# Stores of three phases of a graph network kernel moved from SyncE's queue to ScalarE's

## The chip, the cores and the metric

The kernel runs on one core of one Trainium2 chip. The metric is the device time of one execution in microseconds (us), the median of several runs. The core's engines are TensorE (PE, with its weight loads as PEld), VectorE (DVE), ScalarE (ACT), GpSimd (POOL) and SyncE (SP), each with an instruction stream of its own. They wait for each other by semaphores. Transfers run on 16 DMA engines that the whole core shares.

## The reference, cut to what matters

There are 50,000 nodes with 128 features and 12,500 edges `src -> dst`, sorted by `dst`. Four graph layers follow each other, each as `x = layernorm(x + layer(x))`:

```python
x = _layernorm(x + _L0_gnn_ref(x, edge_index, edge_attr_8, ...))       # attention over the edges
x = _layernorm(x + _L1_gnn_ref(x, edge_index, edge_type_16, ...))      # messages, mean, own layernorm
x = _layernorm(x + _L2_gnn_ref(x, node_vec1, src, dst, edge_attr_4, edge_attr_8, ...))  # equivariant
x = _layernorm(x + _L3_gnn_ref(x, edge_index, ...))                    # hypergraph convolution, batch norm
```

The first layer computes a softmax over the edges of each target and a weighted sum of values; the second a relu of a linear map of source features and edge type, averaged per target; the third gated products of source features and edge attributes, summed per target; the fourth two hypergraph convolutions with a batch norm between.

## The kernel before, in words

Nodes that no edge touches follow a formula of their own (class `Dense`), whose work is sprinkled over the phases. What this case is about are the states of the edges' endpoints. Each phase reads a table in memory with one row of 128 floats for each edge's target (rows 0 to 12,499) and one for its source (the next 12,500), and writes the next table: the attention phase reads `x` and writes T1, the message phase reads T1 and writes T2, the equivariant phase reads T2 and writes T3, and the tail phase reads T3. Between two phases stands a barrier of all engines, and SP does not reach it before all stores of its phase have landed (`sp.wait_ge(s_st[i], ...)`).

Each of the three phases handles the edges in 25 chunks (`NC`) of 500 (`CE`), four tiles (`CT`) of 125 (`TP`). For every chunk POOL gathers source rows (helper `gathers`, line 438), PE turns them and multiplies, ACT copies PSUM and applies functions, DVE does the running sums along the sorted edges, adds the residual, and takes statistics of both rows' norms. Then ACT's `root` takes the square root, DVE's `scale` the reciprocal, and ACT's `norm` (`norm2` in the message phase) writes the normalized rows: eight ACTIVATEs into `y[c % 2]`, four for the targets, four for the sources. `y` has two buffers, so the norm of chunk c waits until the stores of chunk c-2 have landed: `need(act, s_st[c % 2], 32 * (c // 2))`. A store of a chunk, `store(c)`, is two DMAs of 250 KB, 500 rows of 512 bytes each.

The order is written out by hand. Every engine has a loop over steps `s`, and in a step it works on several chunks: what stands as `live(s - 3): norm(s - 3)` is done in step s for chunk s-3. A step of one engine may run at another time than the same step of another engine.

- Attention: ACT (loop at L706) does `outF(s-1)`, `targets`, `query`, `sources` of s+2, `norm(s-2)`, `exps(s+1)`, `root(s-1)`. SP (L542) loads bias and penalties of chunk s+2 and a piece of `xT` for the dense part, then `store(s-2)`.
- Message: ACT (L1437) does `outF(s-1)`, `source(s+2)`, a root, `norm1(s-2)`, `message(s+1)`, `dn.squares` (L1022), a root, `norm2(s-3)`. SP (L1303) loads types, masks and target rows, then `store(s-3)`, and behind it `dn.load_turned` (L1012), the `xT` that `dn.squares` reads.
- Equivariant: ACT (L1737) does `source(s+1)` (L1714, `eq_xs`), `features(s+1)` (L1720 and L1721), `norm(s-3)` (L1734), `gate(s+2)` (L1709, `eq_sg`) and `root(s-2)` (L1726, `eq_sd`). SP (L1613) does `load_scalars(s+3)`, `load_attr(s+1)`, `load_mask(s+1)` (`eq_same`, one row spread over 128 partitions), `load_targets(s)` (`eq_z`) and `store(s-4)` (L1610, L1611).

The waits that bind these loops in the equivariant phase: DVE's `hidden(c)` waits for `gate(c)`; PE's `net(c+1)` waits for `hidden(c)`; PE's `turn` stands behind `net`; ACT's `source` waits for `turn`.

Of the kernel before, what the change touches and what calls it, by code (L numbers as in the profile page):

```python
# [27 lines left out]
N, D, E = 50000, 128, 12500  # L28
# [3 lines left out]
CT = 4  # L32
CE = CT * TP
# [437 lines left out]
def live(c):  # L471
    return 0 <= c < NC


def attention_phase(nc, g, K, T, dn):

    with ExitStack() as ctx:
# [40 lines left out]
        @block.sync  # L518
        def _(sp):
            for n in W:  # L520
                sp.dma_start(W[n][:], g[n]).then_inc(s_w, 16)
            sp.dma_start(bo[:], g["rowv"][0:1, :].broadcast_to([TP, D])).then_inc(s_w, 16)
            sp.dma_start(sel[:], g["sel"]).then_inc(s_w, 16)
            sp.dma_start(spread[:], g["spread"]).then_inc(s_w, 16)
            sp.wait_ge(s_init, 2)
            sp.dma_start(srcI[:], g["src_col"]).then_inc(s_w, 16)
            sp.dma_start(dstI[:], g["dst_col"]).then_inc(s_w, 16)

            def load_pen(c):
                need(sp, s_args, c - 1)  # L530
                sp.dma_start(pen[c % 2][:], T["dpen"][:, CE * c:CE * c + CE].broadcast_to([D, CE])).then_inc(s_pen[c % 2], 16)

            def load_bias(c):
                need(sp, s_att, c - 1)
                sp.dma_start(eb[c % 2][0:8, :], g["ea8T"][:, CE * c:CE * c + CE]).then_inc(s_eb[c % 2], 16)

            def store(c):
                sp.wait_ge(s_y, c + 1)
                sp.dma_start(rows_of(T["T1"], CE * c, CT), y[c % 2][:, 0:CT, :]).then_inc(s_st[c % 2], 16)
                sp.dma_start(rows_of(T["T1"], CE * c + E, CT), y[c % 2][:, CT:2 * CT, :]).then_inc(s_st[c % 2], 16)  # L540

            for s in range(-2, NC + 2):  # L542
                if live(s + 2):
                    load_bias(s + 2)
                    load_pen(s + 2)
                    if s + 2 < MA:
                        dn.load_turned(sp, s + 2)
                if live(s - 2):
                    store(s - 2)
            for i in range(2):  # L550
                sp.wait_ge(s_st[i], 32 * ((NC - i + 1) // 2))
# [112 lines left out]
        def _(act):  # L664
# [40 lines left out]

            for s in range(-2, NC + 2):  # L706
                if live(s - 1):
# [531 lines left out]
def message_phase(nc, g, K, T, dn):  # L1239

    with ExitStack() as ctx:
# [35 lines left out]
        def _(sp):  # L1277
# [19 lines left out]

            def store(c):
                sp.wait_ge(s_y, c + 1)
                sp.dma_start(rows_of(T["T2"], CE * c, CT), y[c % 2][:, 0:CT, :]).then_inc(s_st[c % 2], 16)  # L1300
                sp.dma_start(rows_of(T["T2"], CE * c + E, CT), y[c % 2][:, CT:2 * CT, :]).then_inc(s_st[c % 2], 16)

            for s in range(-4, NC + 3):  # L1303
# [4 lines left out]
                if live(s + 2):  # L1308
                    load_targets(s + 2)
                if live(s - 3):  # L1310
                    store(s - 3)
                if live(s + 2):
# [83 lines left out]
        def _(act):  # L1396
# [39 lines left out]

            for s in range(-2, NC + 3):  # L1437
                if live(s - 1):
# [109 lines left out]
def equivariant_phase(nc, g, K, T, dn):  # L1548

    with ExitStack() as ctx:  # L1550
# [32 lines left out]
        def _(sp):  # L1583
# [23 lines left out]

            def store(c):
                sp.wait_ge(s_y, c + 1)
                sp.dma_start(rows_of(T["T3"], CE * c, CT), y[c % 2][:, 0:CT, :]).then_inc(s_st[c % 2], 16)  # L1610
                sp.dma_start(rows_of(T["T3"], CE * c + E, CT), y[c % 2][:, CT:2 * CT, :]).then_inc(s_st[c % 2], 16)  # L1611

            for s in range(-3, NC + 4):  # L1613
# [5 lines left out]
                if live(s):  # L1619
                    load_targets(s)  # L1620
                if live(s - 4):
                    store(s - 4)
            for i in range(2):
# [79 lines left out]
        def _(act):  # L1703
# [32 lines left out]

            for s in range(-2, NC + 4):  # L1737
                if live(s + 1):
# [590 lines left out]
```

## Time and profile before

| | us |
|---|---|
| median of 3 runs | 2735.31 |
| lowest and highest of them | 2714.59 and 3870.19 |
| profiled execution, its time | 2719.83 |
| its span | 2718.0 |
| of it PE, DVE, ACT, POOL busy | 1473.4, 1681.4, 877.7, 1991.1 |

The profile is of one execution. Its page gives the busy time of the engines, the granted clock of TensorE, the traffic of the DMA queues, and the costliest groups of instructions with what ended the idle time before them. The DMA queue of the kernel's SyncE is q1, that of GpSimd q0. A DMA's row gives the time in which the issuing engine was held by it, not the transfer. The phases lie at about 395 to 790 us (attention), 790 to 1236 (message), 1236 to 1612 (equivariant), and from 1612 the tail, which the change leaves alone.

### The profile page before, as it was taken

The numbers are of one execution on the slowest core, as the hardware profiler recorded it, in microseconds if no ns is written. First come the engines' busy times: TensorE is split into PE (matmuls) and PEld (weight loads), VectorE is DVE, ScalarE is ACT, GpSimd is POOL, SyncE is SP. The second block draws the span as 40 slices with busy tenths as digits, with TensorE's granted clock in tenths as the row PEclk, the third lists the DMA queues.
The fourth block names the chain that finished last, engine by engine and source line by source line (L and its number), as shares of the span: only waits on it lengthen the run. The fifth ranks groups of instructions, "written<-read, shape, count | busy, mean of one in ns | idle before, by whom it ended". The sixth has DMA issues, their size and how long they took to land. (4 is left out here: it accounts for less than half of the span.)

```text
span 2718.0 us, 22486 instructions
## 1 busy us (share of the span) xinstructions
PE 1473.4 (54%) x4577; PEld 752.6 (28%) x4577; DVE 1681.4 (62%) x5026; ACT 877.7 (32%) x1963; POOL 1991.1 (73%) x1591
## 2 busy tenths in 40 slices
PE   5677648888725666536777727746663122321111
PEld 1233224444412232212333314422222121221110
DVE  8999937788825777884777745534445244334443
ACT  0111115766724555661566621111111111210000
POOL 5777767777538888845577767778876687887787
PEclk9988969999958788867888869968886555555555
DMA  1111124444344555524466548868887454543331
GB/s 25 17 28 28 20 75 113 131 127 116 81 105 105 129 132 136 139 64 110 103 138 142 126 93 245 258 189 224 236 229 166 103 126 123 123 120 85 79 86 45
DMA packets 357530, 320.56 MB, mean 118 GB/s; under 512 B 107130, under 2 KB 311825, under 8 KB 357378
## 3 DMA queue, kind: packets, MB, share of 16 engines
q1 hardware_dynamic: 256593, 247.94, 33.4%
q0 software_dynamic: 100800, 71.18, 14.1%
q8 instruction: 39, 0.64, 0.1%
q14 instruction: 98, 0.79, 0.1%
HBM read 222.19 MB, written 96.95 MB: 117 GB/s over the span
## 5 line engine op out<-in xcount | busy, mean ns | idle before, releaser
L2025 PE MATMUL tl_pX<-k_ident,tl_ga 125*128 125x125 f32 x400 | 90.1, 367 | 403.6 <-DMA tl_ga<-table_TE,k_s_idxE 223.8
L438 POOL DMA_INDIRECT tl_ga<-table_TE,k_s_idxE x200 | 243.7, 1218 | 63.1 <-issue 56.1
L2136 DVE TENSOR_TENSOR_SCAN tl_S<-tl_same,tl_S,tl_pX 128x500 f32<-128x500 f32 x96 | 120.1, 1251 | 222.7 <-issue 199.9
L438 POOL DMA_INDIRECT eq_ga<-table_T,k_idxS x100 | 125.1, 1251 | 87.0 <-ACT eq_y L1734 60.1
L1234 DVE TENSOR_TENSOR dr_o<-dr_x,tl_pMul 128x512 f32<-128x512 f32 x98 | 67.0, 684 | 193.7 <-DMA dr_x<-x 110.8
L2025 PEld LDWEIGHTS tl_pX<-k_ident,tl_ga 125*128 125x128 f32 x400 | 62.8, 189 | 419.2 <-DMA tl_ga<-table_TE,k_s_idxE 233.5
L438 POOL DMA_INDIRECT ms_ga<-table_T,k_idxS x100 | 147.2, 1472 | 36.5 <-issue 30.2
L1217 PE MATMUL tl_pCon<-dr_BC,dn_cT 128*128 128x512 f32 x196 | 123.1, 714 | 69.7 <-ACT dn_cT L1224 41.2
L438 POOL DMA_INDIRECT at_ga<-x,at_srcI x100 | 129.0, 1290 | 43.3 <-issue 24.0
L1333 POOL DMA_INDIRECT k_pay<-table_ptab,k_clip x100 | 140.2, 1402 | 27.4 <-issue 27.4
L438 POOL DMA_INDIRECT tl_ga<-table_TH,k_send x100 | 125.1, 1251 | 46.0 <-issue 45.4
L438 POOL DMA_INDIRECT at_gb<-x,at_dstI x100 | 128.3, 1283 | 36.2 <-issue 27.4
L263 POOL DMA_INDIRECT table_ptab<-ix_ef,ix_scatI x100 | 122.2, 1222 | 42.5 <-issue 42.5
L1976 POOL DMA_INDIRECT result<-tl_o,k_dst_end x100 | 120.8, 1208 | 40.2 <-issue 38.1
L268 POOL DMA_INDIRECT ix_pq<-table_ptab,ix_src x100 | 122.2, 1222 | 36.9 <-issue 35.2
L438 POOL DMA_INDIRECT tl_ga<-table_T,k_idxS x100 | 125.9, 1259 | 30.9 <-issue 30.9
L1636 POOL DMA_INDIRECT table_S<-k_pay,k_slot x100 | 121.8, 1218 | 30.5 <-issue 30.5
L1976 POOL DMA_INDIRECT result<-tl_o,k_src_end x100 | 121.5, 1215 | 30.5 <-issue 30.5
L1968 POOL DMA_INDIRECT tl_states<-table_T,k_s_idxS x100 | 120.9, 1209 | 30.5 <-issue 30.2
L430 ACT ACTIVATE ix_hiTb<-ix_pT 128x125 bf16<-128x125 bf16 x100 | 27.7, 277 | 270.2 <-PE ix_pT L398 239.3
L1218 PE MATMUL tl_pMul<-dr_BM,dn_cT 128*128 128x512 f32 x196 | 113.2, 662 | 0.0
L2099 ACT ACTIVATE tl_q<-tl_h,k_cols 128x500 f32<-128x500 f32 x25 | 17.8, 711 | 270.4 <-DVE tl_h L2148 270.4
(430 smaller groups left out, 4718.0 us busy)
## 6 DMA issues: line engine op xcount, KB each, us to landing
dr_x<-x SPq DMA_DIRECT2D x97, 256.0 KB
result<-dr_o SPq DMA_DIRECT2D x97, 256.0 KB
dm_xT<-xT SPq DMA_DIRECT2D x32, 768.0 KB
table_T<-at_y SPq DMA_DIRECT2D x50, 250.0 KB
table_T<-ms_y SPq DMA_DIRECT2D x50, 250.0 KB
table_T<-eq_y SPq DMA_DIRECT2D x50, 250.0 KB
tl_same<-table_dsame SPq DMA_DIRECT2D x50, 250.0 KB
table_TE<-tl_y SPq DMA_DIRECT2D x50, 250.0 KB
```

Source lines behind the costliest of these rows:

```text
L263: nc.gpsimd.indirect_dma_start(out=T["ptab1"], out_offset=bass.IndirectOffsetOnAxis(ap=scatI[:, t:t + 1], axis=0), in_=ef[:, t:t + 1], in_ ...
L268: nc.gpsimd.indirect_dma_start(out=pq[:, t, :], out_offset=None, in_=T["ptab"], in_offset=bass.IndirectOffsetOnAxis(ap=src[:, t:t + 1], ax ...
L438: nc.gpsimd.indirect_dma_start(out=buf[:, k, :], out_offset=None, in_=table, in_offset=bass.IndirectOffsetOnAxis(ap=index[:, CT * c + k:CT ...
L1217: nc.tensor.matmul(self.pC[b][:, 0:w], self.cT[:, h % 2, :], self.BC[:, i, 0:w], start=True, stop=True)
L1218: nc.tensor.matmul(self.pM[b][:, 0:w], self.cT[:, h % 2, :], self.BM[:, i, 0:w], start=True, stop=True).then_inc(self.s_mm, 1)
L1234: nc.vector.tensor_tensor(o, x, self.pM[b][:, 0:w], ALU.mult).then_inc(self.s_mul, 1)
L1333: nc.gpsimd.indirect_dma_start(out=K["pay"][:, t, 2:4], out_offset=None, in_=T["ptab"], in_offset=bass.IndirectOffsetOnAxis(ap=K["clip"][: ...
L1636: nc.gpsimd.indirect_dma_start(out=T["S4"], out_offset=bass.IndirectOffsetOnAxis(ap=K["slot"][:, t:t + 1], axis=0), in_=K["pay"][:, t, :], ...
L1968: nc.gpsimd.indirect_dma_start(out=states[:, k, :], out_offset=None, in_=T["T3"], in_offset=bass.IndirectOffsetOnAxis(ap=K["s_idxS"][:, k: ...
L1976: nc.gpsimd.indirect_dma_start(out=T["out"], out_offset=bass.IndirectOffsetOnAxis(ap=index[:, CT * c + k:CT * c + k + 1], axis=0), in_=o[i ...
L2025: last = nc.tensor.transpose(pX[j % 2][:, k * TP:(k + 1) * TP], ga[j % RG][:, k, :], K["ident"][0:TP, 0:TP])
L2136: nc.vector.tensor_tensor_scan(S[i][:], same[j % RM][:], pX[i][:, 0:CE], 0.0 if j % NC == 0 else S[1 - i][:, CE - 1:CE], ALU.mult, ALU.add ...
```

## The change

In each of the three phases `store(c)` goes from SP's block to ACT's, with the same wait, the same two DMAs and the same semaphores. In ACT's loop it stands first in a step, for the chunk one step later than SP had it: `store(s-3)` in attention, `store(s-4)` in message, `store(s-5)` in equivariant. ACT's loops are a step longer for the last store. SP keeps the loads in their order, and the waits for all stores at its end. From the diff, the equivariant phase whole and the others cut to what differs:

```diff
@@ attention, SP @@
-                if live(s - 2):
-                    store(s - 2)
@@ attention, ACT @@
-            for s in range(-2, NC + 2):
+            for s in range(-2, NC + 3):
+                if live(s - 3):
+                    store(s - 3)
                 if live(s - 1):
                     outF(s - 1)
@@ message, SP @@
-                if live(s - 3):
-                    store(s - 3)
                 if live(s + 2):
                     dn.load_turned(sp, MA + s + 2)
@@ message, ACT @@
-            for s in range(-2, NC + 3):
+            for s in range(-2, NC + 4):
+                if live(s - 4):
+                    store(s - 4)
                 if live(s - 1):
                     outF(s - 1)
@@ equivariant, SP @@
-            def store(c):
-                sp.wait_ge(s_y, c + 1)
-                sp.dma_start(rows_of(T["T3"], CE * c, CT), y[c % 2][:, 0:CT, :]).then_inc(s_st[c % 2], 16)
-                sp.dma_start(rows_of(T["T3"], CE * c + E, CT), y[c % 2][:, CT:2 * CT, :]).then_inc(s_st[c % 2], 16)
-
...
                 if live(s):
                     load_targets(s)
-                if live(s - 4):
-                    store(s - 4)
@@ equivariant, ACT @@
-            for s in range(-2, NC + 4):
+            def store(c):
+                act.wait_ge(s_y, c + 1)
+                act.dma_start(rows_of(T["T3"], CE * c, CT), y[c % 2][:, 0:CT, :]).then_inc(s_st[c % 2], 16)
+                act.dma_start(rows_of(T["T3"], CE * c + E, CT), y[c % 2][:, CT:2 * CT, :]).then_inc(s_st[c % 2], 16)
+
+            for s in range(-2, NC + 5):
+                if live(s - 5):
+                    store(s - 5)
                 if live(s + 1):
                     source(s + 1)
                     features(s + 1)
```

ACT's instructions in the middle of the equivariant phase before, from one root to the norm of the same step and on to the next root (`eq_y0` and `eq_y1` are the two output buffers; semaphores are printed under the name that their number had first):

```order
L1726 ACTIVATE eq_sd0<-eq_mv0,eq_eps 125x8 [waits ix_scat]
L1714 ACTIVATE eq_xs<-eq_pX 128x500 [waits ix_tab,ix_carry]
L1720 ACTIVATE eq_sv0<-eq_pX 128x500 [waits ix_plchain,ix_tab]
L1721 ACTIVATE eq_se0<-eq_pQ 128x500
L1734 ACTIVATE eq_y0<-eq_z2,eq_nb0,eq_rs0 125x128 [waits at_gb2,ix_off]
```

The same place in the changed kernel, one step from root to root:

```order
L1719 ACTIVATE eq_sd0<-eq_mv0,eq_eps 125x8 [waits ix_scat]
L1732 DMA table_T3<-eq_y0 125x4x128 [waits ix_ohA]
L1733 DMA table_T3<-eq_y0 125x4x128
L1707 ACTIVATE eq_xs<-eq_pX 128x500 [waits ix_tab,ix_carry]
L1713 ACTIVATE eq_sv0<-eq_pX 128x500 [waits ix_plchain,ix_tab]
L1714 ACTIVATE eq_se0<-eq_pQ 128x500
L1727 ACTIVATE eq_y0<-eq_z2,eq_nb0,eq_rs0 125x128 [waits at_gb2,ix_off]
L1727 ACTIVATE eq_y0<-eq_z2,eq_nb0,eq_rs0 125x128 x3
L1727 ACTIVATE eq_y0<-eq_ga6,eq_nb0,eq_rs0 125x128 x4
```

The store of `eq_y0` and the norm that writes `eq_y0` anew now stand in one step of ACT, with three ACTIVATEs between them; the norm's first instruction waits (`at_gb2`, the semaphore of that buffer's stores) for the two DMAs just ahead of it.

ACT in the middle of the attention phase, before:

```order
L697 ACTIVATE at_sd1<-at_mv1,at_eps 125x8 [waits ix_looked]
L692 ACTIVATE at_oF<-at_pQ,k_cols 128x500 [waits ix_cur,ix_first]
L671 ACTIVATE at_xd<-at_pT 128x500 [waits ix_deg_cols,ix_carry]
L681 ACTIVATE at_q<-at_pQ,k_cols 128x500 [waits ix_cst,ix_deg_cols]
L676 ACTIVATE at_xs1<-at_pT 128x500 [waits ix_in,ix_runs_rows]
L703 ACTIVATE at_y1<-at_z0,at_nb1,at_rs1 125x128 [waits at_stored1,ix_hit]
```

and in the changed kernel:

```order
L690 ACTIVATE at_sd1<-at_mv1,at_eps 125x8 [waits ix_looked]
L701 DMA table_T1<-at_y0 125x4x128 [waits ix_srcb0]
L702 DMA table_T1<-at_y0 125x4x128
L685 ACTIVATE at_oF<-at_pQ,k_cols 128x500 [waits ix_cur,ix_first]
L664 ACTIVATE at_xd<-at_pT 128x500 [waits ix_deg_cols,ix_carry]
L674 ACTIVATE at_q<-at_pQ,k_cols 128x500 [waits ix_cst,ix_deg_cols]
L669 ACTIVATE at_xs1<-at_pT 128x500 [waits ix_in,ix_runs_rows]
L696 ACTIVATE at_y1<-at_z0,at_nb1,at_rs1 125x128 [waits at_stored1,ix_hit]
```

The two DMAs stand ahead of `at_oF`; the buffer that they read (`at_y0`) is not the one that this step's norm writes (`at_y1`).

## Rows read from the trace of the kernel before

**Rows 1.** Busy time by stretch: attention, message, equivariant; then granted clock, DMA share, GB/s.
```profile
core 0: us, PE busy (x) PEld busy (x) DVE busy (x) ACT busy (x) POOL busy (x), PEclk, DMA share, GB/s
395.00:790.00 395.00, 307.39 (x1165) 167.70 (x1163) 300.00 (x799) 246.20 (x431) 259.69 (x205) 0.92 0.40 107
790.00:1236.00 446.00, 235.27 (x586) 109.59 (x586) 319.50 (x1083) 240.57 (x549) 349.00 (x251) 0.76 0.49 118
1236.00:1612.00 376.00, 263.43 (x650) 116.94 (x650) 258.17 (x730) 196.02 (x371) 243.86 (x199) 0.83 0.54 122
```
**Rows 2.** Waits of SyncE: us in total, times, longest.
```profile
SPq L1300 <- ACT ms_y L1434: 231.1, 23, 20.2
SPq L539 <- ACT at_y L703: 155.6, 21, 11.8
SPq L1610 <- ACT eq_y L1734: 13.7, 4, 4.3
```
**Rows 3.** The tile eq_y: issue durations ns (least, median, most); idle time before its ACTIVATEs.
```profile
L1611 SPq DMA_DIRECT2D table_T<-eq_y x25: 664/4556/4848, 1309.8 to 1603.2; - x25
...
  DMA table_T<-eq_y: 29.4, 10
```
**Rows 4.** Timeline of ScalarE, equivariant phase: start, us, instruction, idle before it.
```profile
1381.83 1.64 ACT L1734 ACTIVATE eq_y<-eq_z,eq_nb,eq_rs 125x128 f32<-125x128 f32 x4
...
1388.21 0.30 ACT L1726 ACTIVATE eq_sd<-eq_mv,eq_eps 125x8 f32<-125x8 f32 x1
...
1397.90 1.64 ACT L1734 ACTIVATE eq_y<-eq_z,eq_nb,eq_rs 125x128 f32<-125x128 f32 x4
...
1404.28 0.30 ACT L1726 ACTIVATE eq_sd<-eq_mv,eq_eps 125x8 f32<-125x8 f32 x1
...
1409.02 1.64 ACT L1734 ACTIVATE eq_y<-eq_z,eq_nb,eq_rs 125x128 f32<-125x128 f32 x4
```
**Rows 5.** Timelines of SyncE and ScalarE, end of the equivariant phase.
```profile
1568.52 0.65 SPq L1610 DMA_DIRECT2D table_T<-eq_y  x1
...
1590.58 0.25 SPq L1610 DMA_DIRECT2D table_T<-eq_y  x1
1590.87 0.66 SPq L1611 DMA_DIRECT2D table_T<-eq_y  x1
...
1568.60 1.65 ACT L1734 ACTIVATE eq_y<-eq_z,eq_nb,eq_rs 125x128 f32<-125x128 f32 x4 [0.94 <-DMA table_T<-eq_y]
...
1580.16 1.65 ACT L1734 ACTIVATE eq_y<-eq_z,eq_nb,eq_rs 125x128 f32<-125x128 f32 x4 [8.18 <-DMA table_T<-eq_y]
...
1587.37 1.65 ACT L1734 ACTIVATE eq_y<-eq_z,eq_nb,eq_rs 125x128 f32<-125x128 f32 x4 [3.83 <-DMA table_T<-eq_y]
...
1592.29 1.65 ACT L1734 ACTIVATE eq_y<-eq_z,eq_nb,eq_rs 125x128 f32<-125x128 f32 x4 [1.54 <-DMA table_T<-eq_y]
...
1599.71 1.65 ACT L1734 ACTIVATE eq_y<-eq_z,eq_nb,eq_rs 125x128 f32<-125x128 f32 x4 [4.05 <-DMA table_T<-eq_y]
```
**Rows 6.** The message phase's last store: timeline of SyncE, then its wait at the end.
```profile
1223.59 0.70 SPq L1301 DMA_DIRECT2D table_T<-ms_y  x1
...
SPq L1241 <- DMA table_T<-ms_y: 5.9, 1, 5.9
```
**Rows 7.** Busy time by stretch, as rows 1, two stretches of the equivariant phase.
```profile
1396.50:1399.50 3.00, 3.00 (x5) 1.22 (x4) 2.30 (x17) 2.55 (x7) 1.15 (x1) 0.54 0.73 67
1400.00:1403.00 3.00, 3.00 (x8) 1.33 (x7) 0.00 (x1) 2.95 (x6) 1.33 (x2) 1.00 0.38 112
```
**Rows 8.** Waits of ScalarE in the attention phase.
```profile
ACT at_oF L692 <- PE at_pQ L633: 47.9, 18, 7.8
```
**Rows 9.** Message phase: GpSimd's groups (busy, mean ns, idle before), and ScalarE's wait for xT.
```profile
L438 POOL DMA_INDIRECT ms_ga<-table_T,k_idxS x97 | 143.5, 1479 | 29.6 <-issue 29.6
L1333 POOL DMA_INDIRECT k_pay<-table_ptab,k_clip x100 | 140.2, 1402 | 27.4 <-issue 27.4
...
ACT dm_z L1022 <- DMA dm_xT<-xT: 37.4, 12, 4.9
```

More of the change, by code:

```diff
@@ L535, in load_bias @@
                 sp.dma_start(eb[c % 2][0:8, :], g["ea8T"][:, CE * c:CE * c + CE]).then_inc(s_eb[c % 2], 16)
-            def store(c):
-                sp.wait_ge(s_y, c + 1)
-                sp.dma_start(rows_of(T["T1"], CE * c, CT), y[c % 2][:, 0:CT, :]).then_inc(s_st[c % 2], 16)
-                sp.dma_start(rows_of(T["T1"], CE * c + E, CT), y[c % 2][:, CT:2 * CT, :]).then_inc(s_st[c % 2], 16)
             for s in range(-2, NC + 2):
@@ L704, in norm @@
                 last.then_inc(s_y, 1)
-            for s in range(-2, NC + 2):
+            def store(c):
+                act.wait_ge(s_y, c + 1)
+                act.dma_start(rows_of(T["T1"], CE * c, CT), y[c % 2][:, 0:CT, :]).then_inc(s_st[c % 2], 16)
+                act.dma_start(rows_of(T["T1"], CE * c + E, CT), y[c % 2][:, CT:2 * CT, :]).then_inc(s_st[c % 2], 16)
+            for s in range(-2, NC + 3):
+                if live(s - 3):
+                    store(s - 3)
                 if live(s - 1):
@@ L1296, in load_targets @@
                 sp.dma_start(xt[c % RX][:], rows_of(T["T1"], CE * c, CT)).then_inc(s_xt[c % RX], 16)
[L1298 to L1301, printed above, removed]
             for s in range(-4, NC + 3):
@@ L1435, in norm2, with store @@
                 last.then_inc(s_y, 1)
-            for s in range(-2, NC + 3):
+            def store(c):
+                act.wait_ge(s_y, c + 1)
+                act.dma_start(rows_of(T["T2"], CE * c, CT), y[c % 2][:, 0:CT, :]).then_inc(s_st[c % 2], 16)
+                act.dma_start(rows_of(T["T2"], CE * c + E, CT), y[c % 2][:, CT:2 * CT, :]).then_inc(s_st[c % 2], 16)
+            for s in range(-2, NC + 4):
+                if live(s - 4):
+                    store(s - 4)
                 if live(s - 1):
@@ L1606, in load_targets @@
                 sp.dma_start(z[c % RZ][:], rows_of(T["T2"], CE * c, CT)).then_inc(s_zd[c % RZ], 16)
-            def store(c):
-                sp.wait_ge(s_y, c + 1)
-                sp.dma_start(rows_of(T["T3"], CE * c, CT), y[c % 2][:, 0:CT, :]).then_inc(s_st[c % 2], 16)
-                sp.dma_start(rows_of(T["T3"], CE * c + E, CT), y[c % 2][:, CT:2 * CT, :]).then_inc(s_st[c % 2], 16)
             for s in range(-3, NC + 4):
@@ L1735, in norm, with store @@
                 last.then_inc(s_y, 1)
-            for s in range(-2, NC + 4):
+            def store(c):
+                act.wait_ge(s_y, c + 1)
+                act.dma_start(rows_of(T["T3"], CE * c, CT), y[c % 2][:, 0:CT, :]).then_inc(s_st[c % 2], 16)
[3 more added lines that the diff above has]
+                    store(s - 5)
                 if live(s + 1):
```

## The prediction

> **What bounds the kernel now.** I read first the busy time by stretch, since the change touches three phases and each may have another limit [rows 1]. In attention PE is busy 307 of 395 us and ACT 246; in message POOL leads with 349 of 446; in equivariant no engine leads (PE 263, DVE 258, POOL 244, ACT 196 of 376), so there a loop of waits sets the pace, not an engine's work. Next SyncE's waits, for what the move could free: its stores held it 231.1 us in message, 155.6 in attention, 13.7 in equivariant [rows 2]. These are waits of a queue, worth something only if an engine then waits for a load behind them. The third view is who waits for stores and loads: ACT waits for its own stores in the equivariant phase, 29.4 us in 10 of 25 norms [rows 3], and for `xT` in the message phase, 37.4 us in 12 waits [rows 9]. No engine waits for a store in the other two phases.
>
> Last, ACT's timeline in the equivariant phase [rows 4]. The root ends, ACT takes the next chunk's source and features, and the norm starts: 1404.58 to 1409.02, 4.4 us, in a quick step; 1388.51 to 1397.90, 9.4, in a slow one; most lie between. I call this stretch from the root's end to the norm's start the gap. From the norm's start to the next root's end it is always about 6.7 us (1381.83 to 1388.51, 1397.90 to 1404.58): norm, gate and root back to back, with two table loads. So ACT is on the loop in every step: gate, DVE's hidden, PE's net and turn, source, features, norm, gate. A step is 6.7 us plus the gap.
>
> **The change in the equivariant phase.** SP issued the store of chunk c about when the norm of c+1 started, at a time when the norm of c+2, which needs it landed, was a whole step off. Now ACT issues it right after the root, and the norm of c+2 stands in the same step behind three ACTIVATEs. The gap can no longer be shorter than the time from issue to landing. Call it L; it takes the place of the old gap wherever that was shorter.
>
> What is L? The trace has no store on an ACT queue, so it is bounded by SP's. At the end of the message phase a store's second DMA was issued from 1223.59 to 1224.29 and SP waited 5.9 us on [rows 6], landing at 1230.2; with the first DMA 0.3 us earlier that is L = 6.9, nothing else in the queue, nothing else moving. At the end of the equivariant phase the store issued at 1590.58 released the norm at 1599.71 [rows 5]: 9.1, with part of the store before it still in the queue. In the steady phase, behind two loads in SP's queue, it was 11.6 (issued 1568.52, norm released 1580.16 [rows 5], one of the ten waits counted in rows 3). A queue of ACT's own has no load ahead, which speaks for 6.9. But by the order of SP's loop the mask broadcast starts when DVE's scan ends, some 5 us after the root, so on the last part of the store; there the DMA engines are busy 0.73 at 67 GB/s, against 0.38 at 112 GB/s while only stores run [rows 7]. I take 1.4 us for that meeting: L = 8.3 with loads beside, 6.9 without. The ends 6.9 and 9.1 stay in the range, 11.6 in a rival.
>
> The old gaps, read off the timeline like the two in rows 4, for the 19 norms of chunks 2 to 20 (first norm 1320.89, last 1568.60): five of 4.44, nine that average 6.17 (5.8 to 6.7), one of 7.3, one of 7.8, one of 9.4, two over 14 where DVE does algebra of the dense part. At L = 8.3: 5 x 3.86 = 19.3, 9 x 2.13 = 19.2, 1.0 + 0.5 = 1.5; the others hide it. Sum 40.0. The last four steps have no gate and no source, only norm and root (3.4 us) and then L: 4 x (3.4 + 6.9) = 41.2 against 1599.71 - 1568.60 = 31.1 now, so +10.1. After the last norm ACT issues two stores instead of one, the earlier one no longer gone by then; a store takes the queue 4.9 us (1587.37 to 1592.29, two norms released by stores queued back to back [rows 5]), +4.9. Equivariant: +55. At L = 6.9 the three terms are 18.9 + 10.1 + 4.9 = 34; at 9.1 throughout 52.8 + 18.9 + 4.9 = 77. The 29.4 us that ACT waits today are inside the old gaps and are not gained on top.
>
> **Attention.** The norm of c+2 stands more than a step (14 us) behind the store, so it will not wait at any of these L. What is added is the issue on ACT. SP's pair took 0.25 + 0.66 us and a gap between, 0.95 us, when its queue had room [rows 5], and up to 0.67 + 4.6 when full [rows 3]. I take 1.0, since ACT's queue holds only its own stores, each gone before the next. It stands ahead of `at_oF`, where ACT waits for PE in 18 steps, 47.9 us in all [rows 8]. Where that wait is over 1 us it hides the issue; of the 23 steps with a store, six have none and two have 0.3 and 0.6. Cost: 6 + 0.7 + 0.4 = 7 us. With no cover it would be 23. SP's 155.6 us of waiting go, but nobody waits for its loads: nothing gained.
>
> **Message.** POOL sets the pace: 349 us busy and 57 us of issue gaps (29.6 + 27.4 [rows 9]) over 25 chunks, 16.2 us each, while ACT is busy 240.6 / 25 = 9.6, so 1.0 us more hides. After POOL's last gather about four chunks drain through ACT and DVE by turns; there it shows, about +3. On the other side `xT` is no longer behind a store that waits for `y`, so the 37.4 us shrink, hidden behind POOL except for the lag of the last chunk, about -2. Sum +1, between -6 and +8.
>
> **Skill against trace.** In rows 5 and 6 a lone store moves its 500 KB in 6.9 us and a queued one in 11.6, so the queue ahead matters here. The Trainium skill (DMA: Bandwidth & Descriptors, section Issuing engines are not separate DMA queues) says that DMAs of all engines run on the same 16 DMA engines and that issuing from several saves only sequencer time; by that alone L would stay at 11.6 and the equivariant term would be 129 instead of 55 (this is the second rival below). The DMA share of 0.38 while only stores run [rows 7] speaks against it: one queue does not fill the engines.
>
> **Sum.** 55 + 7 + 1 = +63 on the profiled execution's 2719.8 (span 2718.0 and 1.8 around it): 2783. The median of the runs shown is 2735.3, 0.6% above the profiled one; two of the three runs are at 2714.6 and 2735.3, so I work from 2719.8. What a measurement of this kernel can tell from no change is about 2%, 54 us.
>
> **Rivals.**
> 1. Forecast: own queue, L between 6.9 and 9.1, issue 1 us. Between 34 + 7 + 1 = +42 and 77 + 7 + 1 = +85: 2762 to 2805. Chance 0.60.
> 2. The queue of its own is no queue of its own: stores land as late as in the steady phase now, L = 11.6. Then 5 x 7.16 + 9 x 5.43 + 4.3 + 3.8 + 2.2 = 95 in the middle, 4 x 15.0 - 31.1 = 29 at the end, 4.9 behind, 129 + 8 = +137: 2857. For it: the shared engines; against it: the low share in rows 7. Chance 0.13.
> 3. Issuing is dear on ACT: each pair holds it about 5.3 us as SP's do when its queue is full [rows 3]. In attention 23 x 5.3 less the 47.9 of cover is +74; in message ACT then has 14.9 of 16.2 us, about +15; in equivariant it stays inside L, +55. Sum +144: 2864. Against it: rows 5's 0.95 with room in the queue. Chance 0.09.
> 4. Not slower: the message phase is paced by ACT's step with its `xT` waits, POOL only keeping up with it. Then each of the 12 waits that goes shortens a step, -37 us in all; it decides from where ACT's step with the wait is the longer one, so over 16.2 us. With the low end of the rest, 34 + 7 - 37 = +4: 2724, no change. For it: 3.1 us per wait on the path of the message; against it: POOL shows only issue gaps, no wait for anyone. Chance 0.15.
> 5. Anything faster than -2%: no row offers 54 us. Chance 0.03.
>
> **How the numbers follow.** The forecast's own range straddles the 2% bound of 2774; at L over 7.8 it is slower, and I put 0.38 of its 0.60 there. With rivals 2 and 3 slower is 0.38 + 0.13 + 0.09 = 0.60; same is 0.22 + 0.15 = 0.37; faster 0.03. The range goes from 2740, inside rival 4, to 2858, which takes in rival 2.
>
> **What would show it.** In the equivariant timeline `eq_y`'s first ACTIVATE should have a wait for DMA `table_T<-eq_y` in nearly every step (not 10 of 25), in total some 80 us or more, with norm to norm at 15.0 us where it was 11.1. The DMA rows on ACT should last 0.25 and 0.7 us; 4 us there is rival 3. The attention phase should be some 7 us longer, the message phase unchanged within 8; if the message phase is 30 shorter, rival 4 holds. Norm to norm at 18 us is rival 2. The prediction fails if L is under 6 us or if the clock of TensorE falls enough in the longer steps that the gaps without stores grow past L.

## The result and the profile after

The changed kernel takes 2764.6 us (median of 4 runs, 2756.7 to 2768.9) against 2728.6 for the kernel before (median of 4, the fastest 2714.6). The ratio is 1.014 with a 95% interval of 1.011 to 1.017: slower by about 38 us, which can be told from no change here, but is under 2%. One of the four runs of the kernel before took 3870.2 us, in a slower state that a run falls into now and then; it is counted in the median of 2728.6 but in no ratio here. The forecast of 2783 was 18 us too high, its range held the time, and 0.37 stood on "within 2%", 0.60 on "slower by more".

Where did the time go? The first row of each phase on SyncE divides the span. First the timeline of SyncE in the kernel before, then in the changed one (start, us, instruction; attention, message, equivariant, tail).

```profile
346.21 0.36 SPq L521 DMA_DIRECT2D at_Wq<-Wq  x1
...
778.47 0.36 SPq L1279 DMA_DIRECT2D ms_Wx<-Wmx  x1
...
1231.46 0.36 SPq L1585 DMA_DIRECT2D eq_A<-L1A  x1
...
1611.72 0.36 SPq L1891 DMA_DIRECT2D tl_W<-W  x1
```

```profile
344.45 0.36 SPq L521 DMA_DIRECT2D at_Wq<-Wq  x1
...
784.47 0.33 SPq L1279 DMA_DIRECT2D ms_Wx<-Wmx  x1
...
1247.83 0.33 SPq L1585 DMA_DIRECT2D eq_A<-L1A  x1
...
1643.12 0.36 SPq L1891 DMA_DIRECT2D tl_W<-W  x1
```

The differences of these rows, to the spans' ends at 2718.0 and 2767.1, with the same division of two later profiled executions of the same two kernels ("again"; the labels are in the next section):

| us | ahead of attention | attention | message | equivariant | tail | span |
|---|---|---|---|---|---|---|
| before | 346.2 | 432.3 | 453.0 | 380.3 | 1106.3 | 2718.0 |
| after | 344.4 | 440.0 | 463.4 | 395.3 | 1124.0 | 2767.1 |
| before, again | 344.6 | 430.4 | 453.0 | 379.0 | 1112.3 | 2719.3 |
| after, again | 351.6 | 438.1 | 464.4 | 395.2 | 1114.1 | 2763.4 |
| forecast, difference | 0 | +7 | +1 | +55 | 0 | +63 |

So in these two pairs the three changed phases cost about 8, 10 to 11 and 15 to 16 us (with more executions attention comes to 4, see below). The largest term of the forecast is more than three times too large, the smallest ten times too small, and the 17.7 us of the tail, which no edit touches, were not in it at all.

**Equivariant.** The rows that answer to [rows 3], of the changed kernel: the issues of the store on ScalarE (duration in ns: least, median, most) and ScalarE's idle time ahead of the norm.

```profile
L1732 ACTq DMA_DIRECT2D table_T<-eq_y x25: 257/258/697, 1327.7 to 1633.0; - x25
L1733 ACTq DMA_DIRECT2D table_T<-eq_y x25: 674/2239/3209, 1328.0 to 1633.7; - x25
...
  DMA table_T<-eq_y: 45.1, 12
```

The forecast wanted this wait in nearly every step and 80 us of it; there are 12 with 45.1, against 10 with 29.4. ScalarE's timeline, which answers to [rows 4], says why (ACTq rows are DMAs issued by its sequencer, ACT rows are work of its engine):

```profile
1375.95 0.58 ACT L1702 ACTIVATE eq_sg<-eq_pH 64x500 f32<-64x500 f32 x1
1375.96 0.26 ACTq L1732 DMA_DIRECT2D table_T<-eq_y  x1
...
1386.22 1.26 ACT L1727 ACTIVATE eq_y<-eq_z,eq_nb,eq_rs 125x128 f32<-125x128 f32 x3 [3.52 <-DMA table_T<-eq_y]
1387.01 0.27 ACTq L1732 DMA_DIRECT2D table_T<-eq_y  x1
1387.32 2.53 ACTq L1733 DMA_DIRECT2D table_T<-eq_y  x1
1387.39 0.48 ACT L1727 ACTIVATE eq_y<-eq_z,eq_nb,eq_rs 125x128 f32<-125x128 f32 x1
1387.78 1.63 ACT L1727 ACTIVATE eq_y<-eq_ga,eq_nb,eq_rs 125x128 f32<-125x128 f32 x4
...
1392.61 0.30 ACT L1719 ACTIVATE eq_sd<-eq_mv,eq_eps 125x8 f32<-125x8 f32 x1
```

In the program the store issued at 1387.01 stands behind the root at 1392.61 (`eq_sd`). In the trace it starts at 1387.01, while the engine is on the third ACTIVATE of the norm: five more of the norm, the gate and the root (seven, with two table loads) are ahead of it in the program and not yet begun. The root ends at 1392.91, 5.9 us later. So the sequencer, which issues the DMA, is ahead of the engine, which executes the ACTIVATEs; the DMA's own wait (for a norm of the step before) is met, and it goes out. In other steps it is further ahead:

```profile
1360.33 0.49 ACT L1727 ACTIVATE eq_y<-eq_z,eq_nb,eq_rs 125x128 f32<-125x128 f32 x1
1360.48 0.26 ACTq L1732 DMA_DIRECT2D table_T<-eq_y  x1
...
1366.71 0.30 ACT L1719 ACTIVATE eq_sd<-eq_mv,eq_eps 125x8 f32<-125x8 f32 x1
```

Here seven ACTIVATEs of the norm, the gate and the root, nine in all, are not yet begun (and again at 1417.10 and 1529.55). The Trainium skill (Advanced Engine Details and Errata, section Engine Queue Depths) gives ScalarE a queue of 8 instructions. That fits the row at 1387.01; nine behind the running one are more than it alone explains, and the measurement decides.

From issue to landing, on the other hand, it takes longer than the 8.3 us taken: from 1375.96 to the norm released at 1386.22 are 10.3 us, and in the other seven norms up to 1593.90 that waited for a store 10.4 to 11.8 us (one 7.9). The end of the phase, the rows that answer to [rows 5]:

```profile
1603.72 1.65 ACT L1727 ACTIVATE eq_y<-eq_z,eq_nb,eq_rs 125x128 f32<-125x128 f32 x4 [6.45 <-DMA table_T<-eq_y]
...
1605.60 0.26 ACTq L1732 DMA_DIRECT2D table_T<-eq_y  x1
...
1614.52 0.49 ACT L1727 ACTIVATE eq_y<-eq_z,eq_nb,eq_rs 125x128 f32<-125x128 f32 x1 [7.42 <-DMA table_T<-eq_y]
...
1622.98 0.26 ACTq L1732 DMA_DIRECT2D table_T<-eq_y  x1
...
1629.74 0.49 ACT L1727 ACTIVATE eq_y<-eq_z,eq_nb,eq_rs 125x128 f32<-125x128 f32 x1 [3.70 <-DMA table_T<-eq_y]
```

From issue to release: 8.9 us at 1605.60, and 6.8 at 1622.98, the last one.

**Message.** GpSimd's group that answers to [rows 9], then ScalarE's waits:

```profile
L1326 POOL DMA_INDIRECT k_pay<-table_ptab,k_clip x100 | 151.3, 1513 | 27.4 <-issue 27.4
```

```profile
ACT ms_oF L1409 <- issue: 43.2, 22, 6.2
...
ACT dm_z L1022 <- DMA dm_xT<-xT: 4.4, 5, 1.7
```

The wait for `xT` went as foreseen (37.4 to 4.4 us). In its place ScalarE is idle ahead of `ms_oF`, 43.2 us in 22 steps with no releaser. One such step in its timeline:

```profile
1199.01 3.17 ACT L1427 ACTIVATE ms_y<-ms_h,ms_nb,ms_rs 125x128 f32<-125x128 f32 x8
1202.21 0.26 ACTq L1432 DMA_DIRECT2D table_T<-ms_y  x1
1202.50 0.71 ACTq L1433 DMA_DIRECT2D table_T<-ms_y  x1
1203.31 0.68 ACT L1409 ACTIVATE ms_oF<-ms_pO,dn_dc 128x500 f32<-128x500 f32 x1 [1.13 <-issue]
```

Here the sequencer can't run ahead: the store stands directly behind norm2, on whose end it waits. Only when the engine has finished `ms_y` are the two DMAs issued, and only then is anything given to the empty engine. GpSimd, on the other hand, does not wait for it: its idle time between gathers and adds is 56.9 us in this execution as in the kernel before. What grew is the time of its own instructions, the payload gathers first (140.2 to 151.3 us); experiment 6 comes back to it.

### The profile page after: what moved, and what is told of

The parts are those of the page before. It is cut to its first block and busy times, and to the rows that moved or that the text cites. A ratio compares the mean times of both kernels' runs of the same rounds, so it can differ in the third digit from the quotient of the medians.

```text
span 2767.1 us, 22486 instructions
## 1 busy us (share of the span) xinstructions
PE 1491.6 (54%) x4577; PEld 759.5 (27%) x4577; DVE 1667.3 (60%) x5026; ACT 880.2 (32%) x1963; POOL 2000.8 (72%) x1591
## 5 line engine op out<-in xcount | busy, mean ns | idle before, releaser
L1326 POOL DMA_INDIRECT k_pay<-table_ptab,k_clip x100 | 151.3, 1513 | 27.4 <-issue 27.4
L438 POOL DMA_INDIRECT at_ga<-x,at_srcI x100 | 129.0, 1290 | 43.2 <-issue 23.9
L438 POOL DMA_INDIRECT tl_ga<-table_TH,k_send x100 | 123.9, 1239 | 44.4 <-issue 43.5
```

Of the source, the lines that this page charges most:

```text
L438: nc.gpsimd.indirect_dma_start(out=buf[:, k, :], out_offset=None, in_=table, in_offset=bass.IndirectOffsetOnAxis(ap=index[:, CT * c + k:CT ...
L1326: nc.gpsimd.indirect_dma_start(out=K["pay"][:, t, 2:4], out_offset=None, in_=T["ptab"], in_offset=bass.IndirectOffsetOnAxis(ap=K["clip"][: ...
```

## The experiments

There were twelve runs, two of them the kernel before and the changed one once more. All compute the reference in full. Phases are divided as above.

**1 to 3. Each phase alone.** The diffs are the three parts of the change, each alone on the kernel before.

> Only the attention stores are issued by ScalarE; the message and equivariant phases are as before. If the costs of the three parts simply add, the attention phase is about 8 us longer (432 to 440, the difference of the two profiled executions, forecast 7), message (453) and equivariant (380) stay, and the whole is 2719 + 8 = 2727 to 2735 us. The tail behind the equivariant phase, whose code never changed, took 1106.3 us in the kernel before and 1124.0 in the changed one. Theory V (that is variation from one execution to the next): the tail is anywhere between 1106 and 1124 here, and the clock of TensorE in its first 200 us goes with it. Theory T (a lasting effect of stores on ScalarE's queue in an earlier phase): the tail is near 1124 in a kernel whose equivariant stores are moved and near 1106 here.

> Only the message stores are issued by ScalarE, ahead of the oF activations and behind norm2. Theory M (ScalarE's sequencer stands at the wait for its own norm2, so that oF begins over 1.1 us later in each of the 22 steps, and POOL with its gathers follows): the message phase is 8 to 10 us longer than 453.0, the waits of ScalarE named DMA for the turned tile fall from 37.4 us to about 5, idle time by issue ahead of oF is near 43 us, the whole 2727 to 2732 us. Rival P (POOL's own instructions were slower by chance in the one profiled execution, k_pay 1513 against 1402 ns): the message phase is within 3 us of 453 here and k_pay near 1402 ns. Rival as forecast before (POOL sets the pace, drain +3, waits -2): +1 us. Tail: Theory V anywhere between 1106 and 1124, Theory T near 1106.

> Only the equivariant stores are issued by ScalarE, five steps behind. Theory A (ScalarE's sequencer reaches the DMA while the engine still executes the activations queued before it, so the store starts 5 to 6 us before the root's end, and only what a landing of 7 to 10 us has left over is waited for): the equivariant phase is about 15 us longer than 380.3, gaps between root and norm of 4.4 to 9.8 us, eq_y waits 45 us for DMA. The forecast's assumption (store only after the root) would give 55 us more. Whole: 2719 + 15 = 2734 us by theory A, 2774 by the forecast's. Theory T on the tail: 1124 here, so the whole is near 2750; Theory V: anywhere from 1106 to 1124.

| stores on ScalarE in | ratio (95%) | attention | message | equivariant | tail |
|---|---|---|---|---|---|
| attention | 1.0031 (1.0013 to 1.0049) | 439.3 | 452.1 | 381.1 | 1107.9 |
| message | 1.0053 (1.0033 to 1.0073) | 435.0 | 465.1 | 380.6 | 1115.7 |
| equivariant | 1.0090 (1.0067 to 1.0113) | 436.1 | 452.1 | 396.7 | 1109.6 |

Each part makes its own phase longer and leaves the two others alone: message +12, equivariant +16. The three ratios multiply to 1.0175, a little above the 1.0130 and 1.014 of the whole; with intervals of about 0.002 on each that is at the edge of what chance explains, so whether the parts simply add stays open. Attention has scatter of its own: ten profiled executions in which its code is unchanged took 430.1 to 437.5, on average 434.8; the four with its stores moved took 438.1 to 440.0, on average 439.1. That is +4, where 7 was forecast. Part even of this may be TensorE's clock, which no run here holds fixed: five of the ten had a granted clock of 0.89 or 0.90 in this phase (on average 432.9 us), the other five 0.88 (436.7), and the moved four 0.87 or 0.88. Against the other five, +2 are left. In the message kernel the idle time ahead of `ms_oF` is there again, 45.8 us in 22, and `xT` is down to 3.7 us: Theory M has its rows, though the phase grew by 12 us and not by 8 to 10. Theory T on the tail gets no support: 1109.6 with the equivariant stores moved, 1115.7 with the message stores.

**4. The store held back to the root's end,** as the forecast had assumed. Equivariant phase alone, one line added to its `store`:

```diff
                 act.wait_ge(s_y, c + 1)
+                act.wait_ge(s_sd, min(c + 3, NC))
```

> As the kernel with the equivariant stores alone, but ScalarE's DMA additionally waits for the end of the root of the same step, which is the moment at which the forecast let it start. Theory A: with that head start taken away the whole landing time stands in the gap: gaps of 7.8 to 10.3 us in each of some 20 steps in place of a mean of 7.3, the last steps longer by the same, the equivariant phase 380 + 45 to 65 us, whole about 2770 to 2785 plus what the tail brings. Rival C (the gap is made by the ring or by the loads that run beside, and not by when the store is issued): the phase is as long as with the store free, +15 us within 5.

Measured: ratio 1.0197 (1.0173 to 1.0220), 2776.8 us, the equivariant phase 432.9, that is +52.6 where the forecast had +55. The rows of this kernel, ScalarE's timeline and the idle time ahead of the norm:

```profile
1397.93 0.30 ACT L1719 ACTIVATE eq_sd<-eq_mv,eq_eps 125x8 f32<-125x8 f32 x1
1398.32 0.26 ACTq L1733 DMA_DIRECT2D table_T<-eq_y  x1
1398.61 0.67 ACTq L1734 DMA_DIRECT2D table_T<-eq_y  x1
```

```profile
  DMA table_T<-eq_y: 69.7, 18
```

Now the DMA does start behind the root (0.09 us behind its end; its line is one further down, for the line added), 18 norms wait, and the gaps of chunks 2 to 20 are 7.5 to 10.6 us (one 14.6), with none of the 4.4 us left. Rival C, that the gap doesn't depend on when the store is issued, falls: one wait on the sequencer is worth 36 us of the phase (396.7 to 432.9). What the forecast worked out was the time of this kernel. Issued at this later moment the stores also land sooner: in the 14 of those 19 steps in which the norm waited for one, 7.6 to 10.5 us after the issue, 8.6 on average.

**5. The store one step earlier,** four steps behind in place of five, still on ScalarE, equivariant phase alone:

```diff
-            for s in range(-2, NC + 5):
-                if live(s - 5):
-                    store(s - 5)
+            for s in range(-2, NC + 4):
+                if live(s - 4):
+                    store(s - 4)
```

> Equivariant stores alone on ScalarE, but four steps behind and not five: the DMA of a chunk stands directly behind its norm, gate and root, where SyncE's stood before, so it starts as soon as the eight activations of the norm have ended and ScalarE's sequencer has passed the root. Theory A (only the head start of the store counts, not the queue): the store starts 3.0 to 4 us earlier than five steps behind in the long steps, the equivariant phase is within 6 us of 380 (396.7 with five behind), whole 2724 to 2732. Rival Q (ScalarE's queue, or the two DMAs in ScalarE's row, is itself what costs): the phase stays near 395 or rises, because ScalarE now stands in front of its source and features for the norm's end.

Ratio 0.9980 (0.9966 to 0.9994), phase 371.8: not only no cost, but a phase 8 us shorter than with SyncE. ScalarE's timeline:

```profile
1401.68 1.64 ACT L1727 ACTIVATE eq_y<-eq_ga,eq_nb,eq_rs 125x128 f32<-125x128 f32 x4
1403.33 1.28 ACT L1702 ACT_TABLE_LOAD   x1
1403.35 0.26 ACTq L1732 DMA_DIRECT2D table_T<-eq_y  x1
1403.64 0.80 ACTq L1733 DMA_DIRECT2D table_T<-eq_y  x1
```

The norm ends at 1403.32 and the store goes out 0.03 us later (never more than 1.7 us later in the phase); the waits for it fall to 6.3 us in 3. Rival Q falls: the queue itself costs nothing here.

**6. The message store behind norm1** of the step, where the norm2 that it waits for has long ended:

```diff
-                if live(s - 4):
-                    store(s - 4)
                 if live(s - 1):
                     outF(s - 1)
...
                 if live(s - 2):
                     norm1(s - 2)
+                if live(s - 4):
+                    store(s - 4)
```

> Message stores alone on ScalarE, but behind norm1 of the same step and not ahead of oF, so the wait for its own norm2 is long met when the sequencer comes to it. Theory M (the stop of ScalarE's sequencer at that wait is what cost the message phase its 12 us): the idle time by issue ahead of ms_oF (45.8 us in 22) goes, the phase is back within 3 us of 452, whole 2721 to 2727. Rival X (stores and turned-tile loads on two queues run beside POOL's gathers and slow these): the phase stays at 460 to 465 and the mean of POOL's k_pay near 1500 ns.

Ratio 1.0018 (1.0001 to 1.0035), phase 458.0: of the 12 us 7 are gone and 5 are left. Neither theory holds alone: Theory M foresaw a phase within 3 us of 452, Rival X 460 to 465. The store goes out ahead of the engine, and no idle time by issue is left ahead of `ms_oF`; ScalarE's timeline here:

```profile
1185.45 0.49 ACT L1420 ACTIVATE ms_n<-ms_xu,ms_nb,ms_rs 125x128 f32<-125x128 f32 x1
1185.48 0.26 ACTq L1432 DMA_DIRECT2D table_T<-ms_y  x1
1185.77 0.72 ACTq L1433 DMA_DIRECT2D table_T<-ms_y  x1
1185.85 2.79 ACT L1420 ACTIVATE ms_n<-ms_xu,ms_nb,ms_rs 125x128 f32<-125x128 f32 x7
```

What is left can be split at the end of GpSimd's last payload gather (from the phase's first row) and what drains behind it:

| kernel | GpSimd's gathers and adds, sum | last payload gather ends at | behind it | phase |
|---|---|---|---|---|
| before | 351.1 | 414.6 | 38.4 | 453.0 |
| before, again | 350.7 | 414.6 | 38.4 | 453.0 |
| message stores ahead of `oF` | 353.6 | 420.7 | 44.4 | 465.1 |
| message stores behind norm1 | 355.0 | 418.7 | 39.3 | 458.0 |
| after | 361.0 | 424.5 | 38.9 | 463.4 |
| after, again | 354.2 | 420.4 | 44.0 | 464.4 |
| all three better placed (experiment 11) | 362.6 | 426.2 | 33.5 | 459.7 |

In experiment 6 the drain is back, and the rest (4.1 us) is GpSimd's own instructions being longer by 3.9 us. Ahead of `oF` there are 6 us of drain as well in two of three executions; in the third, the first of the changed kernel, all but 0.5 of the +10.4 us is GpSimd's own time. GpSimd hardly waits for anyone: its idle time between these instructions is 56.8 to 56.9 us in every execution but two, which had one gap of 3.3 (message stores alone) and 2.3 us (after, again). In eight profiled executions with SyncE's stores where they were the sum was 348.3 to 351.1, so the 2.5 to 11.5 us more are no scatter. The split between gathers and drain changes from one execution to the next, the phase less: 463.4 to 465.1 ahead of `oF`, 458.0 and 459.7 behind norm1. So the place of the store is shown to be worth 4 to 7 us; by which path ScalarE's stop reaches the phase is not shown. What makes GpSimd's instructions longer is a matter of meeting, seen in the changed kernel, GpSimd's timeline and then VectorE's:

```profile
869.56 2.04 POOL L1326 DMA_INDIRECT k_pay<-table_ptab,k_clip  x1 [0.18 <-issue]
871.91 1.21 POOL L1326 DMA_INDIRECT k_pay<-table_ptab,k_clip  x1 [0.30 <-issue]
873.43 2.53 POOL L1326 DMA_INDIRECT k_pay<-table_ptab,k_clip  x1 [0.30 <-issue]
```

```profile
869.34 1.25 DVE L1475 TENSOR_TENSOR_SCAN ms_S<-ms_same,ms_S,ms_m 128x500 f32<-128x500 f32 x1
...
873.61 0.66 DVE L1481 TENSOR_TENSOR ms_mean<-ms_S,ms_deg 128x500 f32<-128x500 f32 x1
```

A payload gather takes 1.21 us, or mostly 2.0 to 2.8 when it meets VectorE in an instruction of two SBUF inputs (`ms_S`, `ms_mean`, `ms_xu` from `ms_ga`, `ms_hg`, `ms_h`). All 32 of over 1.6 us of the changed kernel, all 19 of the kernel before and all 30 of experiment 6 overlap one such row of VectorE, and none of the 45, 33 and 54 payload gathers that overlap none is long. (Not every overlap lengthens one: in the kernel before 48 stay short.) The Trainium skill (SBUF — State Buffer, section Who interferes with whom) says that VectorE and GpSimd share one pair of ports as a lock, which an instruction of VectorE with two SBUF inputs takes against one of GpSimd that reads SBUF; the rows agree in that every long one met such an instruction. The payload's gain of long ones is partly paid back by the other gathers, which meet fewer (their sum falls from 147.2 to 138.5 us with the message stores alone), so what counts is only the sum in the table. That the moved store shifts these meetings is read from the traces; no run here changes the meeting alone.

**7. The load of `xT` ahead of the store,** both on SyncE:

```diff
-                if live(s - 3):
-                    store(s - 3)
                 if live(s + 2):
                     dn.load_turned(sp, MA + s + 2)
+                if live(s - 3):
+                    store(s - 3)
```

> All stores on SyncE as before; in the message phase SyncE only issues the load of the turned tile ahead of the store of the same step. It tells the price of the 37.4 us that ScalarE waited for that tile in 12 places. Forecast of the record (POOL sets the pace): the wait goes and the message phase shortens by at most 2 us, whole within 3 us of before. Rival 4 (these waits set the pace of the phase): 25 to 37 us shorter, whole near 2690. It may also be that the wait does not go, because what it waits for is the loading SyncE's own order behind the gather of the types: then the same time and the same 37 us.

Ratio 1.0010 (0.9990 to 1.0031), phase 452.9, and ScalarE's wait for `xT` 2.8 us in 3. So 35 us of waits went and not one microsecond of the phase: the forecast's fourth rival falls, and with it that ScalarE's step sets the pace here.

**8. Three buffers for `eq_y`,** stores on SyncE. `RY` is 3, the semaphores of the store are as many, and `c % RY` picks both:

```diff
-        y = [a.sb(f"y{i}", [TP, 2 * CT, D]) for i in range(2)]
+        y = [a.sb(f"y{i}", [TP, 2 * CT, D]) for i in range(RY)]
```

> Stores on SyncE as before, but three buffers for the normed tile of the equivariant phase in place of two, so that a norm waits for a store two steps back. Theory A (the gap between root and norm is the landing of the store of two norms ago where it exceeds 4.45 us, which DVE's scale takes anyway): the 29.4 us of waits of eq_y for DMA go to nearly 0 and all gaps to about 4.5 us; the phase shortens by 10 to 29 us, 380 to 351 to 370, whole 2695 to 2714. Rival D (where the wait goes, PE's products or the gathers set the pace and the time is taken back in the next step): the waits go, the phase shortens by less than 8 us.

Ratio 0.9992 (0.9972 to 1.0012), waits for the store 3.2 us in 2, phase 375.1, 5 us less. That is Rival D as written (under 8 us), and Theory A's 10 to 29 us fall: 26 of the 29.4 us of waits go, and ScalarE's wait for PE's turned tile (`eq_xs`) grows from 52.8 to 74.1 us. A wait at the norm is mostly time that the step would have waited for somewhere else.

**9 to 11. The two kernels again, and the change with its stores better placed.** The last one is the changed kernel with the edits of experiments 5 and 6.

> The kernel before, once more, to show what differs between two profiled executions of one program: equivariant phase 380 within 2 us, message 452 within 2, attention anywhere from 430 to 437 (six kernels with unchanged attention gave 430.1 to 437.5), the tail anywhere from 1106 to 1116. Ratio 1.000 within 0.003.

> The changed kernel, once more. Theory V (the tail's extra 17.7 us in the first profiled execution were chance, its code is the same in both): tail 1106 to 1116, the phases before it as they were within 3 us (attention 440, message 463, equivariant 395), profiled execution near 2750 to 2758, which is 2719 + 5 + 11 + 16 and up to 7 of the tail. Theory T2 (the three moves together make the tail slower, though none did alone): tail 1120 to 1128 again. Port theory of the message phase: 30 to 32 of POOL's 100 payload gathers over 1.6 us long, against 19 to 21 with the stores on SyncE.

> All three phases store from ScalarE as in the changed kernel, but the message store stands behind norm1 and the equivariant one four steps behind in place of five. Theory A with M: where the store stands is what costs, so the parts add to 1.003 + 1.002 - 0.002: ratio 1.000 to 1.006, equivariant phase 372 to 376, message 456 to 460, attention 437 to 440. Rival S (stores on ScalarE's queue cost by themselves once all three phases do it): ratio of 1.010 or more.

The kernel before against itself: 1.0017 (1.0000 to 1.0034), so differences of 0.2% mean nothing by themselves. The changed kernel: 1.0130 (1.0103 to 1.0157), its phases as in the table at the top. (The profiled execution took 2765.2 us, where 2750 to 2758 was expected; 7 us of that lie ahead of attention.) Its tail is 1114.1 this time: Theory T2 falls, and the tail's 17.7 us in the first comparison were one execution's. Over the 14 profiled executions of this study, whose tails have the same code, it took 1106.3 to 1124.0. Of the payload gathers 27 were long, fewer than the 30 to 32 expected. All three phases on ScalarE, better placed: 1.0015 (0.9995 to 1.0034), attention 439.1, message 459.7, equivariant 371.1. Rival S falls. Of the change's 1.3%, 1.1 points were where two stores stand in ScalarE's row.

**12. The equivariant store at the head of SyncE's step,** all stores on SyncE. Why did moving it nearer help at all? SyncE's timeline in the kernel before, and the row of VectorE that it waited for:

```profile
1405.17 1.82 SPq L1602 DMA_DIRECT2D eq_ev<-ea4T  x4
1409.95 0.34 SPq L1591 DMA_DIRECT2D eq_same<-table_dsame  x1
1410.34 0.33 SPq L1606 DMA_DIRECT2D eq_z<-table_T  x1
1410.71 0.66 SPq L1610 DMA_DIRECT2D table_T<-eq_y  x1
```

```profile
1408.68 1.24 DVE L1785 TENSOR_TENSOR_SCAN eq_S<-eq_same,eq_S,eq_pO 128x500 f32<-128x500 f32 x1
```

The norm of this chunk ended at 1401.07. SyncE stood at the mask load until the scan ended at 1409.92, and the store behind it went out at 1410.71, 9.6 us after the norm's end.

```diff
             for s in range(-3, NC + 4):
+                if live(s - 4):
+                    store(s - 4)
                 if live(s + 3):
                     load_scalars(s + 3)
...
                     load_targets(s)
-                if live(s - 4):
-                    store(s - 4)
```

> All stores on SyncE; only the equivariant store moves, from the end of SyncE's step to its head, ahead of the loads of scalars, attributes and mask. In the kernel before, SyncE stands at the load of the mask (L1591) until VectorE's scan ends, and the store behind it goes out 9.6 to 10.1 us after the norm's end. Theory A (only when the store starts counts, on whichever queue): the store now starts within 2 us of the norm's end, the waits of eq_y for DMA fall from 29.4 us to under 8, the phase is 370 to 375 us as with the store four steps behind on ScalarE (371.8 and 371.1), ratio 0.996 to 0.999. Rival Q2 (the gain of the store four steps behind came from giving it a queue of its own): the phase stays at 379 to 383, or rises because the loads behind the store come later by its 5.3 us of issue.

Ratio 0.9978 (0.9963 to 0.9993), phase 370.7, waits for the store 4.3 us in 2. SyncE's timeline, and its wait at the store from 1300 to 1560 us:

```profile
1397.24 0.33 SPq L1606 DMA_DIRECT2D eq_z<-table_T  x1
1403.04 0.27 SPq L1610 DMA_DIRECT2D table_T<-eq_y  x1
```

```profile
SPq L1610 <- ACT eq_y L1734: 44.3, 17, 5.7
```

It now waits for the norm itself and issues 0.03 us behind its end (once 1.83). Rival Q2 falls: the same phase as with ScalarE's queue. Its ratio is that of experiment 5 (0.9980) within the noise, 6 us under the kernel before, and it needs no store on ScalarE. The interval just leaves out 1, and by the kernel before against itself (1.0017) so small a gain is not beyond doubt; the phase, 380.3 and 379.0 to 370.7, is clearer.

## Why the prediction was right, and where not

**The direction and the whole** came out: slower, by 38 us where 63 was forecast and 42 to 85 was the likeliest case's own range. The chances leaned the wrong way between its two sides of 2%. The total was nearer than its terms, and that is luck: two errors of opposite sign, -40 in the equivariant phase and +10 in the message phase; a base of 2719.8, where the median of the kernel before is now 2728.6; and in the profiled execution 17.7 us of the tail's scatter.

**Equivariant, +55 (measured +15 to +16).** The step that failed is "Now ACT issues it right after the root, and the norm of c+2 stands in the same step behind three ACTIVATEs". The issue is 5.9 us ahead of the root's end in the row shown. The store of chunk 7, a typical one, went out 9.6 us after its norm's end in the kernel before, 12.4 after it in the changed one, and 18.8 when held to the root: the move cost 2.8 us of head start, and the forecast charged 9. Term by term, in the first changed execution: the 19 gaps grew by 8.9 us (forecast 40.0), the last four steps by 4.7 (10.1), and the stretch behind the last norm by 1.4 (4.9). Everything downstream of the false step held: held to the root, the phase is +52.6 against 55. There the gaps grew by 37.4 (40.0), with an L of 8.6 on average where 8.3 was taken; the last four steps grew by 14.6 (10.1; they took 45.7 us where 41.2 was worked out), and the stretch behind the last norm by 1.8 (4.9). That these two errors cancel is luck. The step of 11.1 us given for the kernel before holds for the quick steps only: from norm to norm it was 13.8 us on average there, 14.2 in the changed kernel and 15.7 when held to the root (chunks 2 to 20).

**The double store at the end, +4.9 (measured +1.4):** from the last norm's end to the first row of the tail are 10.2 us (1632.9 to 1643.1) where it was 8.8 before. The store before the last was issued at 1629.97, when the last norm had just begun (1629.74), and not behind it as the forecast had it.

**Attention, +7 (measured +4 by phase; 1.0031, which is +8 us, with 3.5 to 13 as its interval, by time).** The issue pair takes 1.0 us (0.26 + 0.78) as forecast, but here too the sequencer issues it while the engine still works: idle time by issue ahead of `at_oF` is 3.1, 1.1 and 0.8 us in all in three executions with the stores moved. So the uncovered issues that the 7 us were made of are not what was measured, and where the +4 comes from stays open. Its size is inside the scatter of the phase; that 7 came near is luck.

**Message, +1 (measured +10 to +12).** "POOL sets the pace: 349 us busy" took that busy time as fixed; it grew by 2.5 to 9.9 us with the store ahead of `oF`, and in the first changed execution that is the whole loss but 0.5 us. "ACT is busy 240.6 / 25 = 9.6, so 1.0 us more hides" failed too: it priced the issue and not the stop. Behind its own norm2 the sequencer stands until the engine is empty, 43.2 us of idle time in 22 steps, and without that stop 4 to 7 us of the loss go; by which path it reached the phase stays open. The bound of +8 was too low. The drain term (+3) measured +0.5 to +6.0 ahead of `oF`, and +0.9 and -4.9 behind norm1. The xT term was right in that the waits go (37.4 to 4.4) and are worth nothing (experiment 7), and GpSimd, which hardly waits for anyone, did set the pace.

**The rivals.** Rival 2 (L = 11.6) is nearer than thought: in the middle of the phase, issued as early as the changed kernel does it, the store took 10.3 to 11.8 us (one 7.9), so a queue of its own won little there. That agrees with the rule of the Trainium skill cited in the prediction; that it is the loads beside which delay the store is argued. Issued behind the root it took 8.6 on average, and at the end of the phase 6.8 to 8.9. With 11.6 behind the root the phase would have been +129 by the forecast's working; it was +15, as the issue was earlier. Rival 3 (dear issue) fell in its price, 0.26 + 0.78 us (medians) in attention and message, and 0.26 + 2.24 in the equivariant phase, where the engine has work queued meanwhile. Rival 4 fell to experiment 7.

## What to carry to other kernels

Before a DMA is moved to a compute engine's row, ask what its wait is on. If that is long met, the sequencer issues it ahead of the work still queued on the engine, and the engine loses next to nothing (but whoever waits for the landing counts from when the sequencer comes to it, here 2.8 us later than on SyncE and 15 us in all); if it is the instruction directly ahead of it, the engine runs empty for the issue, and everything behind comes later. And look first at what a late store stands behind on its present queue: here a load that waited for VectorE's scan held it, so that it went out about 10 us late, and putting the store ahead of the loads did as much as a well placed store on a queue of its own (370.7 against 371.8 us).

## What the runs showed of the hardware that was not expected

- A DMA issued by ScalarE starts with up to nine ACTIVATEs (and two table loads) ahead of it in the program not yet begun: at 1360.48 with the root's end at 1367.01. One wait that forbids this costs 36 us of this kernel's equivariant phase.
- A store of 500 KB in two DMAs on a queue of its own landed in 10.3 to 11.8 us in the middle of the phase (one in 7.9), with SyncE's loads beside, and in 6.8 to 8.9 us at its end.
- GpSimd's payload gather takes 1.21 us, or mostly 2.0 to 2.8 when it meets an instruction of VectorE with two SBUF inputs; all 81 payload gathers of over 1.6 us in three traces met one, and none of the 132 that met none was long.
- Two profiled executions of one program differed by 10 us in a phase (the tail: 1124.0 and 1114.1). A phase of one execution is an explanation only when it comes again.
